# Conditioned residual maps: the last two pairs stored in five DMAs each

## The reference

```
W0 = weights0[itok_B_0_15]            # (B, 128, 128), 16 maps to pick from
x  = x + einsum('bct,bcd->bdt', x, W0)
W1 = weights1[itok_B_0_31]            # 32 maps to pick from
x  = x + einsum('bct,bcd->bdt', x, W1) + transpose(biases[itok_B_0_31])
```

## Time and profile before

| | us |
|---|---|
| median of 3 runs | 642.69 |
| lowest and highest of the runs | 642.57, 642.69 |
| the profiled execution | 642.87 |
| its span, first to last instruction | 641.1 |
| PE busy | 537.6 |
| ACT busy | 333.2 |
| DVE busy | 329.2 |
| POOL busy | 123.9 |

### The profile page before, as it was taken

One profiled execution on the slowest core, in us unless ns is written; L12 is line 12 of the kernel. 1 busy time (PEld: TensorE's weight loads), 2 busy tenths in 40 slices (PEclk: granted clock), 3 DMA queues, 4 the chain that ended last, 5 costly groups with the idle time before them and its releaser, 6 DMA issues.

```text
span 641.1 us, 6225 instructions
## 1 busy us (share of the span) xinstructions
PE 537.6 (84%) x2308; PEld 234.0 (37%) x2308; DVE 329.2 (51%) x259; ACT 333.2 (52%) x385; POOL 123.9 (19%) x263
## 2 busy tenths in 40 slices
PE   1899999999889888898898888988988988889870
PEld 0344444443334333343333333333433433334330
DVE  0366666665455445545554555455445544554460
ACT  0466666666455455554554555556545555555450
POOL 2222222222121121221221212212212112122000
PEclk9999999999999999999999999999999999999995
DMA  9999999999999999999999999999999999999995
GB/s 359 428 414 430 428 432 429 429 430 432 431 429 432 431 430 431 431 430 431 430 431 431 430 429 432 430 433 429 431 433 428 429 433 430 429 432 430 430 429 255
DMA packets 18931, 271.82 MB, mean 424 GB/s; under 512 B 2241, under 2 KB 2274, under 8 KB 2274
## 3 DMA queue, kind: packets, MB, share of 16 engines
q1 hardware_dynamic: 9504, 137.37, 50.4%
q10 hardware_dynamic: 9410, 134.26, 49.0%
HBM read 137.40 MB, written 134.22 MB: 424 GB/s over the span
## 4 chain that ended last, share of the span: by engine, by line
DMA 73%; PE 20%; DVE 3%; POOLq 0%; issue 0%; ACT 0%; DVEq 0%; POOL 0%; SPq 0%; ACTq 0%
DMA out_dram<-xt 42%; DMA xt<-in_x_dram 30%; PE acc L160 17%; PE acc L155 3%; DVE xt L224 2%; DMA w_sb<-in_w_dram 1%; DVE xt L226 1%; DVEq L39 0%; ACT L246 0%; POOLq L127 0%; POOLq L130 0%; POOL map0T L137 0%; POOL map L138 0%; ACT both L247 0%; ACT both L246 0%
## 5 line engine op out<-in xcount | busy, mean ns | idle before, releaser
L160 PE MATMUL acc<-xt,both 64*128 64x512 f32 x2048 | 471.7, 602 | 70.6 <-DMA xt<-in_x_dram 68.2
L251 ACT ACTIVATE xt<-acc,bias_of 64x1024 f32<-64x1024 f32 x256 | 283.6, 1108 | 272.3 <-PE acc L160 269.9
L224 DVE TENSOR_SCALAR xt<-acc,bias_of 64x1024 f32<-64x1024 f32 x128 | 163.3, 1276 | 279.8 <-PE acc L160 279.8
L160 PEld LDWEIGHTS acc<-xt,both 64*128 64x128 f32 x2048 | 189.5, 187 | 321.5 <-issue 224.1
L226 DVE TENSOR_SCALAR xt<-acc,bias_of 64x1024 f32<-64x1024 f32 x128 | 165.0, 1289 | 1.9
L137 POOL TENSOR_TENSOR map0T<-w0T_sb,ident 128x128 f32<-128x128 f32 x128 | 65.4, 511 | 467.8 <-PE acc L155 456.1
L155 PE MATMUL acc<-map,map0T 128*128 128x256 f32 x256 | 73.3, 409 | 0.9 <-POOL map L138 0.9
L138 POOL TENSOR_TENSOR map<-w_sb,ident 128x128 f32<-128x128 f32 x128 | 65.3, 510 | 0.0
L155 PEld LDWEIGHTS acc<-map,map0T 128*128 128x128 f32 x256 | 43.8, 191 | 52.3 <-issue 47.8
L247 ACT ACTIVATE both<-acc 64x256 f32<-64x256 f32 x64 | 24.2, 378 | 0.7
L246 ACT ACTIVATE both<-acc 64x256 f32<-64x256 f32 x64 | 24.1, 377 | 0.7
(11 more groups left out here) (4 smaller groups left out, 0.4 us busy)
## 6 DMA issues: line engine op xcount, KB each, us to landing
xt<-in_x_dram SPq DMA_DIRECT2D x64, 2048.0 KB, 27.0
out_dram<-xt ACTq DMA_DIRECT2D x64, 2048.0 KB, 40.5
w_sb<-in_w_dram SPq DMA_DIRECT2D x1, 2048.0 KB, 9.3
w0T_sb<-in_w0T_dram SPq DMA_DIRECT2D x1, 1024.0 KB, 4.8
cond_sb<-in_conds_dram ACTq DMA_DIRECT2D x1, 1.0 KB
bias_sb<-in_bias_dram ACTq DMA_DIRECT2D x1, 16.0 KB, 9.4
cond_rep<-in_conds_dram ACTq DMA_DIRECT2D x1, 16.0 KB, 11.1
```

The lines of the kernel that those rows point to most:

```text
L160: return nc.tensor.matmul(acc[:, j * CHUNK:(j + 1) * CHUNK], both[k * HC:(k + 1) * HC, buf, u, :], xt[k * HC:(k + 1) * HC, slot, u * T + j ...
L224: nc.vector.tensor_scalar(xt[0:HC, q % SLOTS, a:a + HALF], acc0[0:HC, a:a + HALF], bias_of[0:HC, 2 * q:2 * q + 1], None, ALU.add)
L251: return nc.scalar.activation(xt[HC:C, q % SLOTS, v * T + a:v * T + a + HALF], acc1[v * HC:(v + 1) * HC, a:a + HALF], ACT.Identity, bias=b ...
```

## The change

The stores of pairs 62 and 63 are divided by partitions into five DMAs each. ACT's queue issues three: partitions 0 to 31, 32 to 35 and 91 to 122. POOL's queue issues two: 123 to 127 and then 36 to 90. Each of the ten DMAs has a semaphore of its own, and ACT and POOL wait at their ends for those that they issued. The other 62 pairs are stored as before.

```diff
+    ACT_TAIL = [(0, 32), (32, 36), (91, 123)]
+    POOL_TAIL = [(123, 128), (36, 91)]
...
+        tail_stored = [[sem(f"tail_stored{q}_{g}") for g in range(5)] for q in range(2)]
...
+            for q in range(PAIRS - 2, PAIRS):
+                pool.wait_ge(hi_out0, q + 1)
+                pool.wait_ge(hi_out1, q + 1)
+                for g, (lo, hi) in enumerate(POOL_TAIL):
+                    pool.dma_start(out_pairs[q, lo:hi, :],
+                                   xt[lo:hi, q % SLOTS, :]).then_inc(tail_stored[q % 2][3 + g], LOAD)
+            for q in range(2):
+                for g in range(len(POOL_TAIL)):
+                    pool.wait_ge(tail_stored[q][3 + g], LOAD)
...
-                act.dma_start(out_pairs[q, :, :], xt[:, q % SLOTS, :]).then_inc(stored[q % SLOTS], LOAD)
+                if q < PAIRS - 2:
+                    act.dma_start(out_pairs[q, :, :], xt[:, q % SLOTS, :]).then_inc(stored[q % SLOTS], LOAD)
+                else:
+                    for g, (lo, hi) in enumerate(ACT_TAIL):
+                        act.dma_start(out_pairs[q, lo:hi, :],
+                                      xt[lo:hi, q % SLOTS, :]).then_inc(tail_stored[q % 2][g], LOAD)
             for q in range(SLOTS):
-                act.wait_ge(stored[q], LOAD * TURNS)
+                act.wait_ge(stored[q], LOAD * (TURNS if q < SLOTS - 2 else TURNS - 1))
+            for q in range(2):
+                for g in range(len(ACT_TAIL)):
+                    act.wait_ge(tail_stored[q][g], LOAD)
```

## The result

| | before | after |
|---|---|---|
| median of the runs, us | 642.69 | 651.93 |
| lowest and highest | 642.57, 642.84 | 650.72, 653.41 |
| profiled execution, us | 642.87 | 653.41 |
| its span, us | 641.1 | 651.6 |

The changed kernel is 9.2 us slower, a ratio of 1.0143 (95% interval 1.013 to 1.0156). The forecast was 640.1 us, in a range from 638.7 to 645.6.

A forecast was written before the change was run, and what follows sets the result against it. A DMA-bound stream ending with one late engine: relieved, it ends at 635.3, the heaviest other at 637.3; plus 0.3 friction, 0.9 to the span's end, 1.8 around it, less 0.18, gives 640.1 us, range 638.7 to 645.6.

The forecast's parts named there:

- What bounds the kernel: Whole kernel: 2 MB loads and stores keep 16 DMA engines busy; one engine finishes alone, 5.9 us behind.
- (a): Pairs 62 and 63: ACT issues three DMAs per pair at 0.34 us each, 0.68 us more per pair, at no cost.
- the last rows queued within 5 us: Last pair: issues cost nothing if its last rows are queued before the 5.0 us of other queued rows run out.
- (b): Pairs 62 and 63: POOL's two issues take 0.68 to 1.8 us, hidden by queued rows; 0.3 us added for friction.
- (d): Last two pairs: the split changes which engine carries which rows, the whole effect; -4.9 to +2.4 us on the late engine.
- 8 x 0.608: Last two pairs: the late engine carries 8 rows fewer at 0.608 us each, so it ends at 635.3, not 640.2.
- the value I take is the lower one, 4 rows per pair: Last two pairs: late engine gets none of POOL's rows, 4 per pair where it had 8, from bounds of 4 to 10.
- the rule that the prediction names: DMAs use the largest engine count up to 16 dividing their partitions, or sometimes on GpSimd all 16, count rounded up.
- rival 2: Last two pairs: late engine gets one of POOL's 5 rows, none of the 55; 639.3 to 640.3 us; chance 0.17.
- Rival 3: Last two pairs: 32-partition pieces read at half speed, rows 1.2 us; +2.0 us, with friction about 645 us; chance 0.25.
- rival 1: Last two pairs: late engine gets five of the 55, 9 rows per pair; +1.2 us, 643.9 us; chance 0.20.
- rival 4: End of kernel: nothing moves, lateness is a delay of that engine, not its queue; chance 0.08 with cancelling effects.

The follow-up runs named there:

- run 3: Kernel before, stores of pairs 62 and 63 in five pieces cut by columns, all 128 partitions each, on ACT's and POOL's queues: 643.01 us, ratio 1.0002.
- run 11: Kernel before, last two pairs stored in four pieces of 32 partitions, every fourth of all 128, on ACT's queue: 642.73 us, ratio 1.0012.
- run 15: Kernel before, last two pairs in four spread pieces of 32 partitions (every fourth), two on ACT's queue, two on POOL's: 642.67 us, ratio 1.0003.
- run 16: Kernel before, last two pairs in five spread pieces of 32, 4, 32, 5 and 55 partitions, all on ACT's queue: 646.1 us, ratio 1.0056.
- run 6: Kernel before, last pair stored in 16 pieces of 8 partitions four apart, on ACT's queue, using eight engines: 647.67 us, ratio 1.0091.
- run 7: Kernel before, last pair: 2304 columns in one 128-partition piece, the other 1792 in 16 spaced 8-partition pieces on eight engines: 644.95 us, ratio 1.0035.
- run 9: Kernel before, last pair: 3072 columns in one 128-partition piece, the last 1024 in pieces of 116 (four engines) and four of 3: 642.15 us, ratio 0.9999.
- run 10: Kernel before, last pair: 3072 columns in one 128-partition piece, the last 1024 in pieces of 125 (five engines) and 3: 647.63 us, ratio 1.0074.
- run 13: Changed kernel with its counts, order and queues kept, but each piece spread at every second or fourth partition: 646.97 us, ratio 1.0058 to the kernel before.
- run 2: Kernel before, last two pairs stored in four pieces of 32 neighbouring partitions, all on ACT's queue: 646.81 us, ratio 1.006.
- run 5: Kernel before, last pair stored in 16 pieces of 8 neighbouring partitions, on ACT's queue, using eight engines: 651.45 us, ratio 1.0128.

## Why the prediction was wrong

**What bounds the kernel: right.** The stream, one DMA engine that ends alone after the others, and nothing else at the end. Up to the stores of pair 62 the profile is the same, and runs 3, 11 and 15 show the same lone engine (share 0.06 from 636 to 640), with even shares and pieces that reach over all partitions.

**(a) Issues on ACT at 0.34 us each: wrong in size, right in effect.** Three took 1.39 us and then 5.90 us. But the engines were busy meanwhile (share 1.08), ACT's next copy was not held up (2.5 us behind the first issue, 2.6 before), and run 11's four spread pieces took 2.63 us of issues at no cost in time. The condition that the prediction set, the last rows queued within 5 us, is what run 16 broke. What holds an issue up was not tried.

**(b) Issues on POOL: within the bounds** (1.21 and 1.02 us for two). The way to the first packet was longer than I allowed. The DMA view of 614.8 to 619.0 has no packet on queue 0; that of 619.0 to 619.4 has the first twelve, 4.2 us after the issue began at 614.84:

```profile
DMA packets 26, 0.23 MB, mean 574 GB/s; under 512 B 12, under 2 KB 12, under 8 KB 12
...
q10 hardware_dynamic: 14, 0.18, 108.6%
q0 software_dynamic: 12, 0.05, 105.4%
```

The cover of 8.7 us of queued rows hid it, and runs 3 and 15 confirm that POOL's part is free.

**(d) Who carries which rows: this step failed, twice.** First, "8 x 0.608": I priced every row at 0.608 us, because all rows of the trace were. That held only since each store had 128 partitions. In the changed kernel a row took 0.86 us from 628.5 to 633.3. Second, "the value I take is the lower one, 4 rows per pair": I chose that the late engine gets none of POOL's rows. Runs 6, 7, 9 and 10 put it fifth, and a fifth engine gets some by either form of the rule that the prediction names: 5 rows per pair by divisors, which is rival 2 with a gain of 3.4 us; 4 + 1 + 4 = 9 by rounding up, a loss of 1.2. The packets on POOL's queue speak for rounding up. Run 15's page and the changed kernel's:

```profile
q0 software_dynamic: 192, 2.10, 0.8%
...
q0 software_dynamic: 224, 1.97, 0.9%
```

Run 15's four pieces of 32 on POOL are 128 rows and 64 small packets, 16 for each DMA. The changed kernel has 120 rows (1.97 MB), so 104 small packets: 64 as there, and 40 more, 20 per pair. That is what fills 5 rows up to 16 and 55 up to 64, 11 + 9; five engines with one row and eleven with five would need no filling. It goes with run 13, which was slower and not faster. That the fifth engine is among those with four of the 55 is still an inference from the order. The range of the rows (4 to 10) holds; the choice inside it had no row of this kernel behind it.

**The rivals.** Rival 3 (pieces of 32 neighbours are slow) was the mechanism, at a chance of 0.25, and its price was too low: 2.0 us for ACT's eight rows doubled. The even, one-queue case measured 4.1 us (run 2), and I had left out POOL's piece of 55 neighbours and that uneven shares add to it (2.1 us with neighbours on one queue, 4.3 with spread pieces on two). I treated the rivals as if one excluded the other; rival 1's direction (more rows on the late engine, +1.2 us by count) probably holds besides. Of the sign I named for rival 3, "packets longer than 0.61 us" was right and "the share from 624.7 to 633 would fall clearly under 0.99" was not: it was 1.08 and 0.92, and what fell was GB/s. Rivals 2 and 4 don't apply. The stated range, 638.7 to 645.6, was also not worked out: its low end lies above the forecast's own 638.2, and its high end follows from no term.

**What stays open.** Why uneven shares cost more than the rows that they add on the late engine (run 13: 4.3 us over run 15, by count 1.2; run 16: 3.4 us over run 11, by count 2.4 for four more rows, and late issues besides). A reading is that engines slip against each other and then meet at one place: rows were longer in both. Another is that the uneven pieces, with a step of 2 and small ranges, are not spread as well as the even ones. No run here separates that.

Why one engine is late in the kernel before is open too. Its page has two small queues of instruction packets, 0.19 MB together:

```profile
q8 instruction: 7, 0.11, 0.1%
q14 instruction: 10, 0.08, 0.0%
```

If one engine carried them all, that would be 7 us of its time (an estimate, 0.19 MB at 26.9 GB/s), close to the 5.9 us that it is late. No run tried it.

Nothing tried beats the kernel before. Run 9 has the lowest median, 642.15 us, ratio 0.9999 (0.999 to 1.0008), which is no difference.

## What to carry to other kernels

In a DMA-bound stretch, look at GB/s divided by DMA share, not at the share: an engine that reads slowly looks as busy as one at full speed. A store that has to be cut is cut by columns, or by a step over all partitions, not into blocks of neighbours; with even shares both were free here, and blocks cost 4 us for 4 MB (loads were not tried). Many pieces on one queue can make the last one late: look at when its issue ends against the rows that are still queued. Before rows are moved off a late DMA engine, find out which one it is (two kernels with pieces on four and on five engines did it) and what the pieces do to everyone's rate.

## What the runs showed of the hardware

- 32 neighbouring partitions against every fourth of 128, all else equal: 646.81 and 642.73 us; 286 and 426 GB/s per share from 628 to 632.
- Eight engines on eight neighbours got 243 and 326 GB/s per share from 632 to 640, on eight partitions four apart 427 and 420 (runs 5 and 6).
- ACT's issue of one store took 0.34 us when its queue held a few large ones; four pieces of 32 took 3.50 and 9.32 us in run 2 (next fence) and 2.85 and 2.63 us in run 11.

```profile
615.88 3.50 ACTq L108 DMA_DIRECT2D out_dram<-xt  x4
624.45 9.32 ACTq L108 DMA_DIRECT2D out_dram<-xt  x4
```

- POOL's first packet came 4.2 us after its issue began, while about 9 us of rows of other DMAs were queued.
- POOL's DMAs of 5 and 55 partitions left 20 small packets per pair more than the 16 of each DMA (224 in all against 120 rows), as if filled up to 16 and 64 rows.
